# A DLRM tower on one core: twelve small tables found by matmuls instead of ten, a finer step order, and weights loaded between the tables

## What is computed

```python
e = jnp.stack([tbl_0[ids[:, 0]], ..., tbl_26[ids[:, 26]]], axis=1)   # 512 x 27 x 128
z = einsum('bnd,bmd->bnm', e, e)[:, c, r]                            # lower triangle: 512 x 351
h = jnp.concatenate([z, dense_ctx], axis=1)                          # 512 x 367
h = jnp.maximum(h @ W_top1 + b_top1, 0.0)                            # 512 x 512
h = jnp.maximum(h @ W_top2 + b_top2, 0.0)                            # 512 x 256
y = h @ W_top3                                                       # 512 x 1
```

## Time and profile before

| what | us |
|---|---|
| median of 3 runs (all: 122.8, 122.35, 122.95) | 122.8 |
| span of the profiled execution, first to last instruction | 119.5 |
| busy: PE / its weight loads | 95.7 / 78.7 |
| busy: POOL / ACT / DVE | 76.5 / 62.0 / 56.6 |

### The profile page before, as it was taken

One profiled execution on the slowest core, in us unless ns is written; L12 is line 12 of the kernel. 1 busy time (PEld: TensorE's weight loads), 2 busy tenths in 40 slices (PEclk: granted clock), 3 DMA queues, 4 the chain that ended last, 5 costly groups with the idle time before them and its releaser, 6 DMA issues.

```text
span 119.5 us, 3361 instructions
## 1 busy us (share of the span) xinstructions
PE 95.7 (80%) x1500; PEld 78.7 (66%) x1500; DVE 56.6 (47%) x68; ACT 62.0 (52%) x90; POOL 76.5 (64%) x81
## 2 busy tenths in 40 slices
PE   4699999999995612994989997967975869767793
PEld 4478686776873401983878976947954749766690
DVE  5199999999999100359599500411000420004200
ACT  4059979997948000339284443266613365701342
POOL 3777777777768777777677677776777776000000
PEclk9999999999999975599999999999999999999999
DMA  3899556366284994321112122121221211000000
GB/s 37 256 255 241 119 188 192 82 204 195 66 214 119 262 283 120 89 59 44 44 49 69 44 62 56 49 66 44 55 60 49 66 49 49 16 5 5 0 5 1
DMA packets 5195, 11.57 MB, mean 97 GB/s; under 512 B 1840, under 2 KB 2352, under 8 KB 5180
## 3 DMA queue, kind: packets, MB, share of 16 engines
q1 hardware_dynamic: 2812, 6.49, 19.9%
q0 software_dynamic: 2368, 4.85, 16.3%
HBM read 11.34 MB, written 0.00 MB: 95 GB/s over the span
## 4 chain that ended last, share of the span: by engine, by line
PE 39%; POOL 24%; issue 13%; ACT 11%; DMA 8%; DVE 3%; DVEq 0%
POOL rows L323 24%; PE turn_ps L384 13%; PE gram_ps L414 10%; PE chain L446 8%; DMA rows<-tbl,ids_sb 7%; ACT rowsT L590 4%; PE chain L462 3%; DVE gram L523 3%; PE turn_ps L397 3%; ACT rowsT L582 2%; DMA ids_sb<-ids 2%; ACT h2T L612 2%; ACT pairs L599 1%; PE chain L429 1%; ACT high L545 1%
## 5 line engine op out<-in xcount | busy, mean ns | idle before, releaser
L323 POOL DMA_INDIRECT rows<-tbl,ids_sb x74 | 75.7, 1023 | 23.5 <-issue 21.9
L503 DVE TENSOR_TENSOR marks<-ids_ps,row_no 125x1024 fp32r<-125x1024 f32 (+1 forms) x34 | 35.3, 1088 | 3.9 <-PE ids_ps L349 3.9
L590 ACT COPY rowsT<-turn_ps 128x512 f32<-128x512 f32 (+2 forms) x18 | 19.1, 1086 | 16.1 <-PE turn_ps L397 16.0
L384 PE MATMUL turn_ps<-marks,high 125*128 125x384 f32 (+2 forms) x64 | 24.9, 394 | 2.2 <-ACT rowsT L590 1.6
L523 DVE STREAM_TRANSPOSE gram<-gram_ps 128x864 f32<-128x864 f32 x4 | 4.3, 1083 | 41.5 <-PE gram_ps L414 41.5
L384 PE MATMUL turn_ps<-marks,low 125*128 125x384 f32 (+2 forms) x64 | 23.3, 368 | 0.0
L414 PE MATMUL gram_ps<-rowsT 128*27 128x27 f32 x1024 | 13.5, 197 | 6.2 <-issue 4.2
L414 PEld LDWEIGHTS gram_ps<-rowsT 128*27 128x27 f32 x1024 | 11.5, 109 | 8.6 <-issue 5.5
L397 PE MATMUL turn_ps<-ident,rows 128*128 128x128 f32 x64 | 11.3, 284 | 7.0 <-DMA rows<-tbl,ids_sb 5.9
L384 PEld LDWEIGHTS turn_ps<-marks,high 125*128 125x128 f32 x64 | 13.0, 203 | 5.3 <-ACT rowsT L590 2.1
L582 ACT COPY rowsT<-turn_ps 128x384 f32<-128x384 f32 (+2 forms) x8 | 8.1, 1018 | 11.2 <-PE turn_ps L384 11.2
(11 more groups left out here) (38 smaller groups left out, 78.1 us busy)
## 6 DMA issues: line engine op xcount, KB each, us to landing
raw<-tbl SPq DMA_DIRECT2D x10, 448.0 KB
rows<-tbl,ids_sb POOLq DMA_INDIRECT x74, 2.6
raw<-tbl SPq DMA_DIRECT2D x10, 52.0 KB
w_sb<-w SPq DMA_DIRECT2D x2, 256.0 KB
w_sb<-w SPq DMA_DIRECT2D x1, 512.0 KB, 10.7
w_sb<-w SPq DMA_DIRECT2D x1, 222.0 KB
ids_sb<-ids SPq DMA_DIRECT2D x1, 37.0 KB, 1.8
zT<-denseT SPq DMA_DIRECT2D x1, 32.0 KB
```

The costliest lines, as they stand in the source:

```text
L323: nc.gpsimd.indirect_dma_start(out=rows[0:n, i % ROW_BUFS, s, :], out_offset=None, in_=tables[PLACES[s]], in_offset=bass.IndirectOffsetOnA ...
L384: last = nc.tensor.matmul(bank[:, 0:n], part[:, i % SPLIT_BUFS, c * D:(c + 1) * D], mark_of(unit, c), start=c == 0 and part is high, stop= ...
L503: nc.vector.tensor_tensor(marks_of(unit), index.to_broadcast([TP, c1 - c0, n]), which.to_broadcast([TP, c1 - c0, n]), ALU.is_equal).then_i ...
L590: nc.scalar.copy(rowsT_f[:, group[0]:group[-1] + 1, b0:b0 + n], src.rearrange("p (f b) -> p f b", b=n)).then_inc(taken, 1)
```

## The change

What it does:

- `FOUND` has twelve tables. Table 17 is found from tile 0, table 25 from tile 1, and the new tables 0 and 3, with 1250 rows (10 chunks, 5 units each), from tile 1. So 66 gathers are left: 21, 15, 15, 15.
- A find is two steps, `("find", j, 0)` and `("find", j, 1)`. `low` is made in two halves (L545 of the new file, 512 columns, for the 1250-row tables 768 and 512), each after its own units.
- ScalarE casts table j+3 right behind the copy of find j, and no longer ahead of the marks.
- Gram is four parts of 32 matmuls with finds, turns, `l1` or `l2` pieces between them. `l1` goes by output block m, `l2` too. A step waits for the last user of its `chain` bank (`chain_free`).
- `fids_r` and `pick` have all 128 partitions instead of 10 (cleared by one more memset).
- The first table is loaded in two column halves, the large parts by ScalarE's DMA queue. Dense values, w1 and w2 are issued behind tables 4 to 7; w1's last block in 96 and 15 rows.
- `warm`: 8 and 6 at the start, none later.

The diff, cut to its core:

```diff
-FOUND = [(1, 0), (2, 0), (8, 0), (12, 0), (15, 0), (17, 128), (18, 128), (22, 128), (23, 128), (25, 256)]
+FOUND = [(1, 0, 8), (2, 0, 8), (8, 0, 8), (12, 0, 8), (15, 0, 8), (17, 0, 8),
+         (18, 128, 8), (22, 128, 8), (23, 128, 8), (25, 128, 8), (0, 128, 10), (3, 128, 10)]
...
+    order = []
+    for j in range(NEEDED[0]):
+        order += [("find", j, 0), ("find", j, 1)] + turns[0][j:j + 1]
+    order += turns[0][NEEDED[0]:]
+
+    h, t = halves, turns[1]
+    order += gram(0, [h[0:1], h[1:2], h[2:3], h[3:4]])
+    order += t[0:1] + [("pairs", 0, 0), ("pairs", 0, 1)] + h[4:5] + l1(0) + h[5:6] + t[1:2] + h[6:9] + t[2:3] + h[9:]
+    order += t[3:]
+
+    t = turns[2]
+    order += gram(1, [[("l2", 0, 0)], [("l2", 0, 1)], t[0:1], t[1:2]])
+    order += [("l3", 0)] + t[2:3] + [("pairs", 1, 0), ("pairs", 1, 1)] + t[3:]
+
+    t = turns[3]
+    order += gram(2, [[x] for x in l1(1)])
+    order += t[0:1] + l2(1) + [("pairs", 2, 0), ("pairs", 2, 1)] + t[1:2] + [("l3", 1)] + t[2:3] + l1(2) + t[3:]
+
+    order += gram(3, [[("l2", 2, 0)], [("l2", 2, 1)], [("l3", 2)], []])
+    order += [("pairs", 3, 0), ("pairs", 3, 1)] + l1(3) + l2(3) + [("l3", 3)]
...
-                    sp.wait_ge(low_ready, k - RAW_BUFS + 1)
+                    sp.wait_ge(low_ready, 2 * (k - RAW_BUFS + 1))
...
+                if 4 <= k < 4 + BLOCKS:
+                    c = k - 4
+                    whole_16 = K_IN[c] // 16 * 16
+                    for p0, p1 in ((0, whole_16), (whole_16, K_IN[c])):
+                        if p1 > p0:
+                            sp.dma_start(w1_sb[p0:p1, c, :], w1[c * P + p0:c * P + p1, :]).then_inc(w1_in, 16)
...
-                if c0 == 0:
-
-                    dve.wait_ge(high_ready, j + 1)
-                    nc.vector.tensor_tensor(low[:, j % SPLIT_BUFS, :], raw[:, j % RAW_BUFS, :],
-                                            high[:, j % SPLIT_BUFS, :].bitcast(F32),
-                                            ALU.subtract).then_inc(low_ready, 1)
+                if c0 in (0, HALF[j]):
+                    subtract(j, int(c0 != 0))
...
+                if kind == "find" and step[2] == 1:
                     b0, n = JOBS[i]
                     act.wait_ge(marks_used, through(UNITS, i))
                     nc.scalar.copy(rowsT_f[:, place_of(i), b0:b0 + n],
                                    ring_bank(step)[:, 0:n]).then_inc(taken, 1)
+                    if i + SPLIT_BUFS < len(JOBS):
+                        split(i + SPLIT_BUFS)
```

More of the change, by code:

```diff
@@ new lines, in steps, with gram, l1, l2 @@
+    halves = [("find", j, h) for j in range(NEEDED[0], len(JOBS)) for h in range(2)]
+    def gram(i, between):
+        out = []
+        for q in range(GRAM_PARTS):
+            out += [("gram", i, q)] + between[q]
+        return out
+    def l1(i):
+        return [("l1", i, m) for m in range(M1)]
+    def l2(i):
+        return [("l2", i, m) for m in range(M2)]
+    order = []
+    for j in range(NEEDED[0]):
+        order += [("find", j, 0), ("find", j, 1)] + turns[0][j:j + 1]
+    order += turns[0][NEEDED[0]:]
@@ L336, in use_ring, with chain_free @@
                 return ring_bank(step)
+            def chain_free(step):
+                at = [s for s, _ in CHAIN].index(step)
+                before = [s for s, bank in CHAIN[:at] if bank == CHAIN[at][1]]
+                if not before:
+                    return
+                kind, i, *part = before[-1]
+                if kind == "pairs":
+                    pe.wait_ge(z_ready, 2 * i + part[0] + 1)
+                elif kind == "l1":
+                    pe.wait_ge(h1_ready, M1 * i + part[0] + 1)
+                elif kind == "l2":
+                    pe.wait_ge(h2_ready, M2 * i + part[0] + 1)
+                else:
+                    pe.wait_ge(y_ready, i + 1)
             def spread_ids(j):
@@ L368, in _ @@
                 kind, i = step[:2]
-                in_ring += kind in ("find", "turn")
+                in_ring += step in RING
                 if kind == "find":
                     _, n = JOBS[i]
-                    bank = use_ring(step)
-                    pe.wait_ge(low_ready, i + 1)
-                    for unit in units_of(i):
+                    half = step[2]
+                    bank = use_ring(step) if half == 0 else ring_bank(step)
+                    pe.wait_ge(low_ready, 2 * i + half + 1)
+                    for unit in units_in(i, half):
                         _, c0, c1 = unit
-                        if c1 == ROWS_EACH and i + 2 < len(JOBS):
+                        if c1 == CHUNKS[i] and i + 2 < len(JOBS):
                             spread_ids(i + 2)
@@ L402, in _ @@
                     b0, n = TILES[i]
-                    half = step[2]
-                    if half == 0:
+                    part = step[2]
+                    if part == 0:
                         pe.wait_ge(taken, in_ring)
@@ L409, in _ @@
                             pe.wait_ge(regrouped, i)
-                    for g in range(half * STRIP // 2, (half + 1) * STRIP // 2):
+                    for g in range(part * STRIP // GRAM_PARTS, (part + 1) * STRIP // GRAM_PARTS):
                         for s in range(n // STRIP):
@@ new lines, in _ @@
+                    for c in range(BLOCKS):
+                        if m == 0 and c < 2:
+                            pe.wait_ge(z_ready, 2 * i + c + 1)
+                        last = nc.tensor.matmul(chain[:, m % 2, m * P:m * P + n],
+                                                w1_sb[0:K_IN[c], c, m * P:(m + 1) * P],
+                                                zT[0:K_IN[c], c, b0:b0 + n],
+                                                start=c == 0, stop=c == BLOCKS - 1)
+                    last.then_inc(l1_done, 1)
@@ L470, in _ @@
+                    for c in range(M1):
+                        if m == 0:
+                            pe.wait_ge(h1_ready, M1 * i + c + 1)
+                        last = nc.tensor.matmul(chain[:, m % 2, m * P:m * P + n],
+                                                w2_sb[:, c, m * P:(m + 1) * P], h1T[:, c, 0:n],
+                                                start=c == 0, stop=c == M1 - 1)
+                    last.then_inc(l2_done, 1)
                 elif kind == "l3":
                     n = TILES[i][1]
+                    chain_free(step)
@@ L515, in _ @@
                         mark(unit)
-                if kind == "gram" and more[0] == 1:
+                if kind == "gram" and more[0] == GRAM_PARTS - 1:
                     n = TILES[i][1]
```

219 lines of the change are left out of this document (106 added, 113 removed).

## The result

| what | before | the change |
|---|---|---|
| median of 4 runs each, on one chip | 122.9 us (122.35 to 123.28) | 132.7 us (131.03 to 133.33) |
| ratio, 95% interval | | 1.084 [1.066, 1.103] |
| span of the profiled execution | 119.5 us | 129.2 us |

What follows compares the result with a forecast made beforehand. VectorE's list was taken to decide the first regrouping, PE being busiest later. Gram 1 at 77.2 plus 44.1 gave a span of 121.3, 1.8 over 119.5; the median 122.8 + 1.8 = 124.6 us, range 120.8 to 128.0.

Steps and rivals of the forecast that it cites:

- VectorE's list: Marks and half `low` ahead of the first regrouping: 46.3 us from 6.4, so that regrouping at 52.7, where it stood at 49.87.
- So PE follows VectorE to 37.3: Ahead of gram 0: PE's job takes 4.5 us, VectorE's 4.6 to 5.8, so VectorE is not short; gram 0 starts at 40.0.
- the cover of 1.1 us for job 9's: Behind gram 0: job 9's ids ready at 49.2, 1.1 us before VectorE asks at 50.3; the whole cover for late table 8.
- the clock term: PE's wait ahead of the first pairs: half a find at half clock, 1.3 us more, bounds 0 and 3; gram 1 at 77.2.
- Gram 2 to gram 3: Gram 2 with three quarters of `l1`, pairs, ScalarE's work, `l3`, then `l1`, turn and copy: 16.5 us.
- Gram 3 to the end: Gram 3 with `l2` and `l3` 5.9 us, then 10.5 from the last regrouping to the end as before: 16.4 us.
- the fall at the end: Rival, chance 0.15: the clock falls behind gram 3, where no warm matmuls stand; +2.7 us, 127.3.
- So my sum holds none of them: PE's 4.2 us of waits inside gram, placed where two instructions per 10 ns pass are eaten, were taken to go entirely.
- the waits that stay: Rival, chance 0.08: PE's waits in gram stay, +4.2 us, 128.8.
- The clock stays up in the wait: Rival, chance 0.15: no clock loss of 1.3 us in PE's wait ahead of the first pairs, 123.3.
- The same chain, shorter: Rival, chance 0.15: half `low` at 0.53, free shape changes, no clock loss; 119.6 to 121.5, gram 1 to end 42 or less.
- Gathers were the bound: Rival, chance 0.07: 10.7 us of GpSimd's gathers go, gram 3's stage grows by 1.4; total 113.5.

Runs made afterwards that it cites:

- the filled and the unfilled profiles: Filled: the change plus warming matmuls in PE's waits, total unknown (disturbed runs), 38.4 us behind the second regrouping. Unfilled: the change itself, 43.1 us there, ratio 1.084.
- ten tables: The change's new order with the ten tables of the kernel before, without fillings: 123.6 us, ratio 1.015 to the kernel before.
- the early-weights kernel: The kernel before with only dense values, w1 and w2 issued behind tables 4 to 7: 121.35 us against 121.28, ratio 0.997.
- `l1` late: The change with `l1` of tile 0 moved behind the finds of tile 1: 132.2 us, ratio 1.085 to the kernel before.
- the filled ten: The change's order with the ten tables of before, plus warming matmuls in PE's waits: 123.1 us against 121.5 for the kernel before, ratio 1.012.

## Why the prediction was wrong

The direction and most of the mechanism held; two terms of the sum did not. By its own steps, forecast span 121.3, measured 129.2, 7.9 us to explain:

- **VectorE's list: right, 46.4 for 46.3**, though it began 0.9 us earlier than taken. "So PE follows VectorE to 37.3" failed: PE's last find pass before gram 0 ended at 39.2, its jobs took 5.0 us (30.19 to 35.23) and not 4.5, so gram 0 started at 41.78 and not at 40.0, and its first part and the eight find passes behind it ran at the lower clock. The ids of job 8 stand behind them and came 2.80 us late; the cover of 1.1 us for job 9's was none, they were 0.25 late. First regrouping 54.94 for 52.7: **+2.2**.
- **Regrouping to job 10's marks:** 9.8, for 8.7 and the clock term of 1.3, which belongs here: **-0.2**. The size of that term came right by luck. It was priced for half a find; slow were two find passes and above all `l1`, 4.17 for 3.1, for which the bound of 3 was named.
- **Job 10's marks to gram 1:** 15.5 for 14.5, **+1.0**. PE waits three times there for ScalarE's copies, 0.57, 1.01 and 1.43 us; the sum had its finds with a copy waited for twice, and does not show them one by one.
- **Gram 1 to gram 2:** 11.35 for 11.2, right; PE's wait of 1.55 in it cost nothing.
- **Gram 2 to gram 3:** 18.06 for 16.5, **+1.6**: two of the four gram parts and two of the four quarters of `l1` ran at the lower clock (0.97 for 0.74, 1.65 for 0.94), 2 x 0.23 + 2 x 0.71 = 1.9.
- **Gram 3 to the end:** 19.51 for 16.4, **+3.1**: 1.59 is PE's wait ahead of the last gram pass, and 1.9 the lower clock behind it (12.36 from the last regrouping, where the sum had 10.5); the passes ahead came 0.4 short.

So the step that failed is the clock term: one stretch at 1.3 us was priced, with the fall at the end as a rival of 0.15 (+2.7). There were four, and they were counted one at a time. The two behind gram 1 make 3.5 of the 7.9 us (1.6 and 1.9), and the filled and the unfilled profiles, one at full clock and one not, show 3.4 for them. Ahead of gram 1 only the timeline speaks: `l1` 1.2, eight find passes at 0.32 for 0.175, a gram part 0.3, 2.7 us of added passes, of which 1.3 was priced. No undisturbed run has all stretches filled with twelve tables, so what the clock costs in the total is not measured; with ten tables filling them changed the total by nothing that can be told (1.012 for 1.015), since gathers and a wait of PE's own came in its place.

The row read for the clock, that pauses of 1.5 us inside gram left it at 1.00, was one outcome and was taken for a rule. In the same trace a wait of 1.85 us left it up too; in the early-weights kernel 1.54 at the same pass was followed by the lower clock, and so was the 1.59 here. With `l1` late, waits of 1.28 and 0.28 stand where the change has 1.55 and 0.24, and the clock stays up. The length of a wait alone does not tell.

The second is PE's own wait in the last gram. "So my sum holds none of them" was wrong by 1.59 us, of 4.2 before. More instructions of other shapes between the gram passes did not remove it. The Trainium skill (Runtime: NRT & Kernel Launch, Instruction fetch mechanics) has the crossing of a block mostly hidden; two waits of 1.6 us in 129 can be called that, and one of them was hidden behind another wait, but the other stands on the chain that sets the end. Whether it is a fetch is not shown: warming passes far ahead moved it, and no row names its cause.

The rivals: the clock at the end came true, in size 1.9 for 2.7; the waits that stay came true in part, 1.6 for 4.2. Each had its price alone, and they came together. "The clock stays up in the wait" did not come true, it fell at 59.0. "The same chain, shorter" neither: gram 1 to the end took 48.9 us and not 42, and a half `low` 0.60. "Gathers were the bound" was as unlikely as said: with 66 the last is issued at 90.95, 18.7 us ahead of gram 3, and nobody there waits for it. That is the gain that the change bought, and it bought what nobody was waiting for: eight gathers of GpSimd, for 15 us more of VectorE (71.5 for 56.6) and 9 more of PE (105.0 for 95.7, a part of it passes at the lower clock), nearly all ahead of gram 1, where the chain runs through both. With ten tables the gathers do stand close behind, as the early weights and the filled ten show. No version that ran undisturbed beats the kernel before.

## What to carry to other kernels

Price the clock by what the new order does to PE, not by one old row: write down PE's gaps, stage by stage, add up the cost of the passes behind all of them at half speed, and take the sum as a bound of the forecast, since the same gap left the clock up in one kernel and was followed by the lower one in another. Before relieving an engine, see who waits for it last: GpSimd's share of the chain was the largest, and the stage that paid for relieving it was another. Where ids, marks and products are made by turns, ask what stands ahead of the next ids on PE: gram in parts put 6.94 us of waiting into VectorE with the same ten tables. And when a fix moves its own stage but not the end, look at once for the queue that now ends last: here a gather every 1.25 us stood some 2 us behind.
